# Where the values' matmuls stand between the score tiles of a 16-head attention

## What is computed

```python
q = ((x @ wq + bq) * HEAD_DIM ** (-0.5)).reshape(b, s, N_HEADS, HEAD_DIM)
k = (x @ wk + bk).reshape(...);  v = (x @ wv + bv).reshape(...)
p = softmax(einsum('bqhd,bkhd->bhqk', q, k), axis=-1)
o = einsum('bhqk,bkhd->bqhd', p, v).reshape(b, s, d) @ wo + bo
```

## Time and profile before

| | |
|---|---|
| median of three runs | 2586.51 us |
| the profiled execution: its own time | 2590.43 us |
| its span | 2588.6 us |
| mean granted TensorE clock over the span | 0.904 |
| busy, PE / VectorE (DVE) / ScalarE (ACT) / GpSimd (POOL) | 80% / 73% / 52% / 26% |
| first and last exponential of this attention (L1271) | 703.7 and 1178.7 us from the start |

### The profile page before, as it was taken

The page is one execution under the profiler, slowest core; times in us unless marked ns, Lnnn a source line. Parts: engine busy times, 40 slices in busy tenths (PEclk is TensorE's granted clock), DMA queues, the critical chain, the costliest instruction groups (busy, mean ns, idle before and its releaser), DMA issues. The chain is left out here.

```text
span 2588.6 us, 41389 instructions
## 1 busy us (share of the span) xinstructions
PE 2061.5 (80%) x13856; PEld 1198.8 (46%) x13856; DVE 1877.6 (73%) x4504; ACT 1344.9 (52%) x2902; POOL 682.9 (26%) x591
## 2 busy tenths in 40 slices
PE   6777877775588888883991574999999989999995
PEld 2333333322244444442440342666666666666663
DVE  5999999997366666651215486888887688888865
ACT  5666656652144343331443102777777377777731
POOL 1343333332001122112342023332331133323211
PEclk8898998888699999995995687999999999999998
DMA  7000000000100000001423322000000000000000
GB/s 258 0 3 2 5 4 4 5 4 15 43 5 13 14 15 16 13 13 55 147 71 108 118 93 65 1 2 1 1 2 1 1 1 2 1 2 2 1 13 21
DMA packets 81555, 73.91 MB, mean 29 GB/s; under 512 B 11412, under 2 KB 66336, under 8 KB 81121
## 3 DMA queue, kind: packets, MB, share of 16 engines
q1 hardware_dynamic: 77248, 63.21, 8.0%
q0 software_dynamic: 4096, 8.06, 0.9%
HBM read 37.76 MB, written 33.86 MB: 28 GB/s over the span
## 5 line engine op out<-in xcount | busy, mean ns | idle before, releaser
L766 DVE TENSOR_TENSOR_SCAN m_hs<-m_da,m_bu 128x1024 f32<-128x1024 f32 x128 | 296.3, 2355 | 0.3
L463 PE MATMUL m_ps_y_ps<-m_prod,m_ident 128*128 128x512 f32 x512 | 281.5, 678 | 4.9 <-DVE m_prod L776 4.9
L1271 ACT ACTIVATE a_pt<-a_ps_s 128x1024 f32<-128x1024 f32 x128 | 131.1, 1024 | 280.2 <-PE a_ps_s L1045 264.9
L1395 DVE TENSOR_REDUCE a_mpad<-a_ps_s 128x4 f32<-128x1024 f32 x128 | 156.9, 1226 | 164.1 <-PE a_ps_s L1037 164.1
L1037 PE MATMUL a_ps_s<-a_kT,a_qT 32*128 32x256 f32 x1024 | 197.3, 461 | 71.4 <-DVE a_mpad L1395 64.1
L2768 ACT ACTIVATE l_pe<-l_ps_s,l_nbias,l_qs 128x192 f32<-128x192 f32 (+1 forms) x512 | 244.8, 487 | 13.9 <-DVE l_nbias L2940 11.7
L373 POOL TENSOR_TENSOR m_bu<-m_dtu,m_bsb 128x1024 f32<-128x1024 f32 x64 | 151.5, 2367 | 358.2 <-ACT m_bsb L614 224.6
L2524 PE MATMUL l_ps_s<-l_kT,l_qT 128*128 128x192 f32 (+1 forms) x1024 | 221.4, 321 | 0.0
L1045 PE MATMUL a_ps_s<-a_qT,a_kT 32*128 32x256 f32 x1024 | 194.8, 459 | 2.6 <-ACT a_pt L1271 2.6
L2524 PEld LDWEIGHTS l_ps_s<-l_kT,l_qT 128*128 128x128 f32 x1024 | 155.0, 191 | 51.0 <-issue 39.8
L623 ACT ACTIVATE m_da<-m_dt,m_a_neg 128x510 f32<-128x510 f32 x256 | 168.0, 714 | 4.1 <-DVE m_hs L766 2.6
(11 more groups left out here) (323 smaller groups left out, 4928.0 us busy)
## 6 DMA issues: line engine op xcount, KB each, us to landing
slots<-m_void SPq DMA_DIRECT2D x16, 516.0 KB, 5.9
e_xs<-slots SPq DMA_DIRECT2D x16, 258.0 KB
ys<-m_void SPq DMA_DIRECT2D x8, 512.0 KB, 6.6
e_w<-in_w SPq DMA_DIRECT2D x16, 256.0 KB, 3.5
e_yy<-ys SPq DMA_DIRECT2D x16, 256.0 KB, 5.3
m_xt<-in_L_attn_x SPq DMA_DIRECT2D x8, 256.0 KB, 3.1
x<-m_xo SPq DMA_DIRECT2D x8, 256.0 KB, 2.2
a_xn<-x SPq DMA_DIRECT2D x4, 512.0 KB, 4.8
```

The source lines that it names most:

```text
L463: last = pe.matmul(y_ps[h][:, :], ident[:, :], prod[s % 2][:, h, :], start=(s == 0), stop=False)
L766: dve.tensor_tensor_scan(hs[s % 2][:, :, :].rearrange("p h t -> p (h t)"), da[s % 4][:, :, :, :].rearrange("p h q t -> p (h q t)"), bu[s % ...
L1395: dve.tensor_reduce(dst, s1[:, :, :], AX.X, ALU.max, negate=True).then_inc(max_rd, 1)
```

## The change

The callback that issues `weigh` is called at the end of `scores` and of `last_scores`, behind both pairs, and no longer between them. The wait for `pair_mm` stays, and now follows the first four matmuls directly. E still follows what `scores` issues. No instruction is added or removed, and no other queue is touched.

```diff
-                def scores(b, p, t, b1, p1, t1, between):
+                def scores(b, p, t, b1, p1, t1, after):
 
                     wait_s2(b, t)
                     wait_s1(b1, t1)
                     s1_pair(p1, t1, (0, 2))
                     s2_pair(p, t, (1, 3)).then_inc(pair_mm, 1)
-                    between()
                     pe.wait_ge(pair_mm, LEAD + 8 * b + t + 1)
                     s1_pair(p1, t1, (1, 3)).then_inc(s1_mm, 1)
                     s2_pair(p, t, (0, 2)).then_inc(s2_mm, 1)
+                    after()
...
-                def last_scores(b, p, t, between):
+                def last_scores(b, p, t, after):
 
                     wait_s2(b, t)
                     s2_pair(p, t, (1, 3)).then_inc(pair_mm, 1)
-                    between()
                     pe.wait_ge(pair_mm, LEAD + 8 * b + t + 1)
                     s2_pair(p, t, (0, 2)).then_inc(s2_mm, 1)
+                    after()
```

More of the change, by code:

```diff
@@ L1155, in body, with after @@
                     for t in range(8):
-                        def between():
+                        def after():
                             if t > 0:
@@ L1162, in body @@
                         if t < 8 - LEAD:
-                            scores(b, p, t, b, p, t + LEAD, between)
+                            scores(b, p, t, b, p, t + LEAD, after)
                         elif last < 2:
-                            scores(b, p, t, b + 1, q, t + LEAD - 8, between)
+                            scores(b, p, t, b + 1, q, t + LEAD - 8, after)
                         else:
-                            last_scores(b, p, t, between)
+                            last_scores(b, p, t, after)
                         if t == 0 and last < 2:
```

## The result

The changed kernel takes 2554.67 us, the median of four runs (2547.09 to 2557.44), against 2587.34 for the kernel before on the same chip (four runs, 2586.35 to 2589.72). The ratio is 0.9867, 95% interval 0.9847 to 0.9886: 33 us or 1.3% less. The profiled execution took 2557.44, its span is 2555.6 (2588.6 before), and the mean granted clock is 0.910 (0.904).

A forecast was written before the change was run, and what follows sets the result against it. VectorE's row maximum and TensorE's score matmuls hand one buffer back and forth, neither full. Blocks 3 to 13 give 33.5, 0 to 2 3.2, 14 1.0, 15 2: 39.7, taken as 38; 2586.5 - 38 = 2549 us, range 2540 to 2574.

The forecast's parts named there:

- the forecast case: Whole kernel: the reordering gains 38 us and the clock stays up, 2549 us; chance 0.60.
- A to B: Each slot, TensorE: second half of the score matmuls (B) starts 0.79 us behind the first (A), before 1.22.
- W behind B: Each slot, TensorE: the values' matmuls (W) start 0.64 us behind the second half of the score matmuls (B).
- E behind W: Each slot, TensorE: extra matmuls (E: queries, keys, transposes, `maxima`) start 0.57 us behind the values' matmuls (W).
- The slots: Eight slots of a block without late signals, each the larger of VectorE's chain and TensorE's: 26.50 us against 27.56.
- The loss in slot 4: Slot 4: `put_max` waits for later `maxima`, idle 0.3 us; the slot takes 3.62, losing 0.29.
- Hold and clock: Blocks 3 to 13: late signals in slot 1 (hold) cost 0.99 us, before 1.40; low clock's 1.58 goes.
- The drain: Around the two score halves: the tiling rule would save one drain, some 0.57 us a block, 9 in all.
- Blocks 0 to 2: First three blocks: each gains 1.06 us, 3.2 together.
- Blocks 14 and 15: Last two blocks: block 14 gains 1.0 us; block 15 gains 2, some 0.3 in each of seven slots.
- the hold catches the new wait: Slot 1: the bare wait for `pair_mm` is held, the clock falls; costs 26 of 38 us, 2575; chance 0.13.
- B of slot 1 late by more than 1 us: Slot 1: sign of a wrong forecast, the second half of the score matmuls starting more than 1 us late.

The follow-up runs named there:

- e4: Changed kernel with the values' matmuls called at the end of every slot, behind the extra matmuls too: 2542.53 us, ratio 0.9814.
- e6: Kernel before with its 64 indirect DMAs and the waits for them left out: 2544.45 us, one run.
- e7: Changed kernel with its 64 indirect DMAs and the waits for them left out: 2524.75 us, one run.
- e8: Kernel before with the eight transposes of slot 1 issued twice: 2576.54 us, ratio 0.9944.
- e3: Changed kernel with the values' matmuls back between the two score halves in slot 1 alone: 2548.32 us, ratio 0.9836.
- e2: Changed kernel with GpSimd's sends (indirect DMAs) moved ahead of its power: 2532.72 us, ratio 0.9779.
- e1: Kernel before with GpSimd's sends (indirect DMAs) moved ahead of its power: 2580.75 us, ratio 0.9961.
- e12: Changed kernel with sends ahead of the power and, in slot 3 alone, the values' matmuls behind `project` and `maxima`; chip with late signals: 2542.26 us, ratio 0.9813.
- e5: Changed kernel with the values' matmuls last in every slot and GpSimd's sends ahead of its power: 2544.68 us, ratio 0.9821.

## Why the prediction was right

The forecast was 2549 us and the measurement 2554.67, inside the range and inside the forecast case's own 2541 to 2558.

- *A to B.* Forecast 0.79, measured 0.80; the row of `first_scores` was the right one to take. W behind B (0.64) and E behind W (0.57) hold exactly.
- *The slots.* Without the hold, block 2 of the kernel after goes 3.94, 3.04, 2.91, 2.91, 3.64, 2.91, 3.27, 3.94, against 3.93, 3.02, 2.91, 2.91, 3.62, 2.92, 3.26, 3.93. The loss in slot 4 was real, with the cause named (e4 takes it back); only the idle before `put_max` is 0.20 and not 0.3.
- *Hold and clock.* Forecast 0.99 for the hold in place of 1.40, measured 27.54 - 26.57 = 0.97. TensorE's idle before the next A is 0.51 and not the forecast 0.92, because B itself was held and 0.49 of the idle now lies before B. The clock stays up in blocks 4 to 13. Of the 34.95 us of blocks 3 to 13, the order gives 303.23 - 292.26 = 11.0 (e6 and e7). The holds cost 17.25 before (e8 less e6) and 302.93 - 292.26 = 10.7 after, 6.6 less: some 0.4 in each block, and the 2.0 at the start of block 14, which the prediction left as it was, shrinks to 0.3. The clock gives the 17.4 that are left (337.88 less the 320.48 of e8), as forecast. e8 also shows what the prediction could only take for likely, that an idle stretch of 0.90 us behind the hold leaves the clock up (its own rows had 0.55); in e3 1.11 to 1.17 did so too.
- *The drain.* The Trainium skill, TensorEngine Tiling (Array Packing), Key Properties, has a change of tiling mode drain the engine. The saving that this might have brought (slots 7 and 0 at 3.79, 2540 us) isn't in the trace: they take 3.94. That doesn't say that no drain exists.

Mis-sized terms:

- *Blocks 0 to 2*, -5.15 and not -3.2: block 0 has no work of a block before it, so its slots 0, 4 and 6 take 3.35, 2.91 and 2.91 in the kernel after, and it gains 2.8 us by itself. The prediction gave it an ordinary block's gain.
- *Blocks 14 and 15*, forecast -3 and measured +3.5, are the largest miss. The order alone gives what was forecast: 27.11 + 25.35 in e6 against 25.55 + 23.4 in e7, 3.5 less. What was left out is that the hold moves. Before, it lay in the last slot of block 14 (step 4.33 between exponentials in place of 3.33). Now it lies in slot 1 of block 15, where the rival "the hold catches the new wait" came true. The kernel after:

```profile
1112.84 0.48 PE L1037 MATMUL a_ps_s<-a_kT,a_qT 32*128 32x256 f32 x2 [0.84 <-ACT a_pt L1271]
...
1113.13 0.97 POOL L981 DMA_INDIRECT slots<-a_h2n,a_dest  x1 [0.30 <-issue]
...
1115.11 0.80 PE L1037 MATMUL a_ps_s<-a_kT,a_qT 32*128 32x256 f32 x2 [1.55 <-remote]
```

B is 2.27 behind A with TensorE idle for 1.55; its own matmul already runs at the lower level (0.80 us for 0.48), and the clock stays at 0.50 past the last exponential. (By the prediction's own list, B of slot 1 late by more than 1 us was a sign of its being wrong; it appears in this one block.) The wait and the idle time alone don't bring this about, though. The same slot in e2:

```profile
1102.63 0.48 PE L1037 MATMUL a_ps_s<-a_kT,a_qT 32*128 32x256 f32 x2 [0.84 <-DVE a_mpad L1395]
...
1102.93 0.97 POOL L981 DMA_INDIRECT slots<-a_h2n,a_dest  x1 [0.30 <-issue]
...
1104.88 0.48 PE L1037 MATMUL a_ps_s<-a_kT,a_qT 32*128 32x256 f32 x2 [1.54 <-PE a_ps_s L1045]
```

Here too B is 2.25 behind A, after the same idle time and with the DMA at the same place, and it runs at the full clock. The block takes 22.0, its step over the held slot 4.37 in place of e7's 2.91. So the held wait itself costs 1.46 us, and the low clock in the kernel after 32.72 - 22.0 = 10.7.

The last block loses the clock in every kernel here, also where nothing is sent: e6 and e7 fall to 0.50 some 16 and 14 us behind the block's first exponential, with no idle stretch above 1.41 us in or beside the block, and don't come back before its last exponential. Beside the hold the fall comes earlier, if it comes: within 4 us of that first exponential the clock falls in the kernel before, e1 and e8 (TensorE idle for 2.2 us), the kernel after and e12 (1.55 and 1.54), and e4 and e5 (1.3), and not in e2 (1.54) and e3 (0.87). In the kernel before, e4, e5 and e8 it was back within 4 us; in the kernel after, e1 and e12 it stayed down. Two windows of e4:

```profile
1109.00:1112.00 3.00, 3.00 (x24) 1.77 (x16) 1.70 (x4) 1.40 (x2) 0.00 (x0) 0.50 0.00 0
1112.00:1122.00 10.00, 9.17 (x76) 4.18 (x68) 3.57 (x14) 3.57 (x5) 0.72 (x1) 1.00 0.05 13
```

What decides between these three outcomes is open; it alone is worth 10 us.

- *Outside this stretch*, 3.6 us were lost (2.1 before the first exponential, 1.5 behind the last) that nothing ties to the change. The first exponential of the kernels here lies between 703.1 and 705.8, and what follows the last one, where all rows are sent, takes 1407.3 to 1411.4.

The step of the rival was wrong in size and place: it was priced for eleven blocks, in which B of slot 1 was held for 0.4 and lost nothing, and not for the last.

The whole of it: order alone -19.6 (e6 and e7), shorter holds in blocks 3 to 13 -6.6, clock kept there -17.4, hold and low clock of the last two blocks +7.0, together -36.6 from the first exponential to the last, and +3.6 outside, which is the 33.0 between the spans. That the total came out so near is in part luck: up to block 13 the change gained 3.4 us more than forecast, behind it and outside 10.1 less.

Open is what holds the signals, and why one of four chips is free of it. Open too is which of the four DMAs does it; the fourth alone, with the row maximum 1.9 to 2.0 us behind it, doesn't fit all rows. In block 10 of e2 and e5, and for B in slot 1 of the kernel after, the release is only 0.46 to 0.53 behind the fourth, and 1.73 to 1.80 behind the third. Open is also the kernel after's own scatter: 2547.09 in one of its runs, 2554.53 to 2557.44 in the others. Block 15 at the full or the lower clock is a difference of about that size, but there is no trace of the short run.

## What to carry to other kernels

Work that is moved out of a wait uncovers the wait. Before the move, look in each kind of slot, those of the last block too, at what may delay that signal. If a burst of indirect DMAs makes signals late, put it where the engine that waits has long work queued behind its last signal (e2), and not just ahead of a bare wait (e5). And price a stall with the clock that it may cost: filling 0.9 us of TensorE's idle with useless transposes made a kernel 13 us shorter (e8).

## What the hardware showed that was not expected

- While GpSimd issues indirect DMAs, signals raised by TensorE reach VectorE, ScalarE and TensorE itself late. In slot 1 the row maximum's release was 1.9 to 2.0 us behind the issue of the fourth DMA, before and after the change, and the price 1.40 us in the kernel before; other signals were let go 1.73 to 1.80 behind the third. It went away with the DMAs (e6, e7) and moved with them (e1, e2, e5, e12).
- It was so on three of the four chips of the experiments, and absent on the fourth, where the kernel before is 33 to 37 us shorter. One and the same change has the ratio 0.9867 on a chip with the hold and 0.9932 on that one.
- In the full blocks the clock fell after each of the ten idle stretches of 1.77 to 1.84 us in the kernel before, after one of ten of 1.53 to 1.60 in e1, and after none of 0.51 (kernel after), 0.89 to 0.96 (e8) or 1.11 to 1.17 (e3). In the last block stretches of 1.55 in the kernel after and 1.54 in e2 had opposite outcomes.
- Once down in the last block of the kernel after, the clock stayed at the lower level past the last exponential, with TensorE busy for 9.75 and more of every 10 us; in e4 it was down with TensorE busy for 3.00 of 3 us, and came back. A high busy share thus says nothing of which level TensorE is at.
